# Two maxima per step ahead of the exponentials: a reordered attention stage on one core

## The reference, cut to what matters

```python
q = _rmsnorm(_rope(q), q_norm_w)
k = _rmsnorm(_rope(k), k_norm_w)
scores = jnp.einsum('bqgtd,bqgsd->bqgts', q, k) * scale
scores = jnp.where(mask[None, None, None], scores, NEG)
attn = jax.nn.softmax(scores, axis=-1)
out = jnp.einsum('bqgts,bqgsd->bqgtd', attn, v)
out = out.transpose(0, 3, 1, 2, 4).reshape(Bx, Tx, QPG * N_KV * D_HEAD)
return out @ wo.T
```

## Time and profile before

| | us |
|---|---|
| median of 3 runs (lowest, highest) | 1922.25 (1918.28, 1922.78) |
| profiled execution, its own time | 1921.04 |
| its span | 1919.1 |
| PE busy in the span | 1778.8 (93%) |
| DVE busy | 1530.7 (80%) |
| ACT busy | 1355.5 (71%) |
| POOL busy | 920.5 (48%) |

### The profile page before, as it was taken

The page is one execution under the profiler, slowest core; times in us unless marked ns, Lnnn a source line. Parts: engine busy times, 40 slices in busy tenths (PEclk is TensorE's granted clock), DMA queues, the critical chain, the costliest instruction groups (busy, mean ns, idle before and its releaser), DMA issues.

```text
span 1919.1 us, 35529 instructions
## 1 busy us (share of the span) xinstructions
PE 1778.8 (93%) x10789; PEld 1275.9 (66%) x10789; DVE 1530.7 (80%) x3377; ACT 1355.5 (71%) x3865; POOL 920.5 (48%) x1544
## 2 busy tenths in 40 slices
PE   3999999999999977999997999999999999989998
PEld 2777887887887866877775666666655665654443
DVE  5788888888888856567657899998999888986665
ACT  1567777677677653444445999999998999986765
POOL 1222322322322310032238999999898999983200
PEclk9999999999999988999997999999999999999999
DMA  3311111111111000000000000000000000004454
GB/s 98 95 44 40 34 45 39 34 45 39 34 45 39 25 1 1 1 1 1 1 1 1 2 2 2 2 2 2 2 2 1 2 2 2 2 7 177 189 216 165
DMA packets 30520, 69.05 MB, mean 36 GB/s; under 512 B 14108, under 2 KB 14748, under 8 KB 28028
## 3 DMA queue, kind: packets, MB, share of 16 engines
q1 hardware_dynamic: 30332, 66.78, 10.6%
HBM read 45.12 MB, written 2.36 MB: 25 GB/s over the span
## 4 chain that ended last, share of the span: by engine, by line
PE 33%; DVE 10%; ACT 9%; issue 6%; POOL 4%; DVEq 0%; ACTq 0%; POOLq 0%
ACT apb L1460 5%; PE ps L65 4%; PE ps L67 3%; PE ps L66 3%; PE ps L1218 3%; PE ps L1777 3%; PE ps L1201 3%; PE ps L1189 3%; PE ps L1228 2%; POOL apb L1574 1%; DVE atq L1281 1%; PE ps L1763 1%; PE ps L1184 1%; DVE amx L1321 1%; ACT aqT L1449 1%
## 5 line engine op out<-in xcount | busy, mean ns | idle before, releaser
L1460 ACT ACTIVATE apb<-ps,amx 128x128 f32<-128x128 f32 x1024 | 360.5, 369 | 23.6 <-DVE amx L1321 22.8
L1574 POOL TENSOR_TENSOR apb<-apb,arc 128x512 f32<-128x512 f32 x256 | 268.2, 1048 | 28.4 <-DVE arc L1329 27.4
L1460 ACT ACTIVATION_READ_ACCUMULATOR apb<-ps,amx 128x1 f32 x1024 | 214.4, 209 | 0.0
L1336 DVE COPY apT<-ps 128x512 f32<-128x512 f32 x256 | 172.6, 674 | 51.2 <-PE ps L1201 47.9
L583 POOL TENSOR_TENSOR h0h<-h0h,const 128x1 fp32r<-128x1 f32 x256 | 46.7, 218 | 338.8 <-DVE h0l L479 338.8
L65 PE MATMUL ps<-h0h,w123h 128*128 128x512 f32 x512 | 203.2, 397 | 0.0
L67 PE MATMUL ps<-h0h,w123l 128*128 128x512 f32 x512 | 202.5, 396 | 0.0
L66 PE MATMUL ps<-h0l,w123h 128*128 128x512 f32 x512 | 202.5, 395 | 0.0
L479 DVE SCALAR_TENSOR_TENSOR h0l<-ps,h0h 128x1024 fp32r<-128x1024 f32 x128 | 156.1, 1219 | 46.5 <-ACT h0h L383 46.5
L1201 PEld LDWEIGHTS ps<-const,apb 128*128 128x128 f32 x1024 | 109.8, 141 | 121.3 <-issue 90.9
L1321 DVE TENSOR_REDUCE amx<-ps 128x4 f32<-128x512 f32 x256 | 174.3, 681 | 4.6 <-PE ps L1189 4.3
(11 more groups left out here) (325 smaller groups left out, 5030.8 us busy)
## 6 DMA issues: line engine op xcount, KB each, us to landing
h<-gates SPq DMA_DIRECT2D x8, 2048.0 KB, 7.0
atq<-gates SPq DMA_DIRECT2D x8, 2048.0 KB, 7.0
x0k<-x0h SPq DMA_DIRECT2D x128, 72.0 KB
x<-in_x SPq DMA_DIRECT2D x32, 192.0 KB, 2.6
x0k<-x0l SPq DMA_DIRECT2D x64, 72.0 KB
x0k<-x0h SPq DMA_DIRECT2D x64, 48.0 KB
out<-akT SPq DMA_DIRECT2D x16, 128.0 KB, 1.9
x0k<-x0l SPq DMA_DIRECT2D x32, 48.0 KB
```

The source lines that it names most:

```text
L1336: ve.tensor_copy(pT[:, 4 * k:4 * k + 4, :], ps[:, TB, :].rearrange("p (h t) -> p h t", h=4)).then_inc(S["pT"], 1)
L1460: last = ac.activation(pb[:, i % 2, head, :], ps[:, SB[n % 3], h * T:(h + 1) * T], ACT.Exp, bias=mx[:, k, h:h + 1], accum_out=sm[:, i % 2, ...
L1574: po.tensor_tensor(p, p, rc[:, i % 2, 4 * k:4 * k + 4].unsqueeze(2).to_broadcast([T, 4, T]), ALU.mult).then_inc(S["pn"], 1)
```

## The change

Four edits. DVE takes both maxima of a step in the even slot, and in the odd slot the reciprocals of both slots, with the rotation between them; the sum of squares moves one slot on. ACT reads the rotated sum of the queries in SBUF (`qr`) for its squares, where it read the projection in PSUM, and waits for POOL's addition (`S["qr"]`) for it. On ACT the exponentials stand at the head of the odd slot, and in the even slot `keep_x` and the square come behind them. PE's projection waits for the rotation of the one before (`S["rope"]`), which is now the last to read the bank, where it waited for the square.

```diff
         def project(m):
             i, h = m // 2, m % 2
             if m >= 1:
-                pe.wait_ge(S["sq"], m)
+                pe.wait_ge(S["rope"], m)
...
-            if 0 <= u < PARTS:
-                maximum(u)
-            if 0 <= u - 1 < PARTS:
-                recip(u - 1)
+            if u % 2 == 0:
+                if 0 <= u < PARTS:
+                    maximum(u)
+                    maximum(u + 1)
+            else:
+                if 0 <= u - 1 < PARTS:
+                    recip(u - 1)
+                if u in at_q:
+                    rope_q(at_q[u])
+                if 0 <= u < PARTS:
+                    recip(u)
+                if u - 2 in at_q:
+                    sum_q(at_q[u - 2])
             if u in at_pt:
                 p_copy(at_pt[u])
-            if u in at_q:
-                rope_q(at_q[u])
-            if u - 1 in at_q:
-                sum_q(at_q[u - 1])
...
-            ac.wait_ge(S["rope"], m + 1)
+            ac.wait_ge(S["qr"], m + 1)
             if i >= 1:
                 ac.wait_ge(S["ssq"], m - 1)
-            ac.activation(sqb[:, h, :], ps[:, QB, :], ACT.Square).then_inc(S["sq"], 1)
+            ac.activation(sqb[:, h, :], qr[i % 2][:, h, :], ACT.Square).then_inc(S["sq"], 1)
...
+            if u % 2 == 1 and 0 <= u < PARTS:
+                exps(u)
             if u - 1 in at_pv:
                 keep_o(at_pv[u - 1])
-            if u - 1 in at_q:
-                square(at_q[u - 1])
             if u - 1 in at_qt:
                 keep_q(at_qt[u - 1])
             if u in at_rms:
                 rms_q(at_rms[u])
-            if u in at_xt:
-                keep_x(at_xt[u])
...
-            if 0 <= u < PARTS:
+            if u % 2 == 0 and 0 <= u < PARTS:
                 exps(u)
+            if u in at_xt:
+                keep_x(at_xt[u])
+            if u - 1 in at_q:
+                square(at_q[u - 1])
```

## The result

The changed kernel takes 1989.47 us (median of 4 runs, 1988.60 to 1990.28) against 1921.39 before (median of 4, with one run more than the table above): a ratio of 1.0357, with a 95% interval of 1.0339 to 1.0375. The forecast was 1988. The profiled execution spans 1988.3 us, 69.2 more than before. One single run in all that follows, of e7, was a slow one (2324.47 us at a granted clock of 0.745, where its others had 0.97), and e7's number is the median of its other three.

A forecast was written before the change was run, and what follows sets the result against it. It took a ring of four engines, ordered by handovers, to bound the attention stage. 43.7 + 2.07 + 0.49 + 0.87 + 0.4 gave a 47.5 us period against 43.3; times 15.9, +67 on 1921: 1988, range 1955 to 2015.

The forecast's parts named there:

- No instruction gained or lost, all is order: Attention stage: 256 maxima, 256 reciprocals and 128 squares stay as before; the change is only order and waits.
- The loop of 5.46 us a step through the second reciprocal: ACT and DVE: DVE's reciprocal awaits its own slot's exponentials, closing a loop of 5.46 us a step, 43.7 for eight.
- E0: ACT's exponentials of the even slot, 1.37 us in the loop's sum.
- E1: ACT's exponentials of the odd slot, 1.37 us in the loop's sum.
- Extras on the loop: Once a period: 2.07 DVE pieces, 0.49 copy of inputs, 0.87 unhidden ACT pieces, 0.4 late transposes; period 47.5 us.
- the stage's +67: Attention stage: a period longer by 4.2 us, times 15.9 periods, adds 67 us to the kernel's time.
- The square's slower read: ACT's square from SBUF instead of PSUM: +0.034 us a step, 4.4 us if on the ring, 0 if not.
- PE's removed waits give nothing: Projection's 18.3 us wait for squares goes, at most 1.3 us of PE a period; costed at zero gain.
- Small loss: Rival: DVE's part of the loop is hidden, ACT's path bounds; +0.7 a period, 1932 us; chance 0.10, in-between included.
- PE's clock: Rival, larger loss: a twentieth of the stage at half clock with PE 85% busy, +26 us, 2014; chance 0.10.
- The signs: Expected in the profile: periods 47 to 48 us, reciprocals waiting every step, logarithm waits near 0.6, PE waiting at L1218.
- The gain: Rival: PE, 93% busy, sets the ring, so its shrunken waits save 37 us, giving 1884; chance 0.03.

The follow-up runs named there:

- e7: The changed kernel with the query edit alone undone: square reads the projection in PSUM, projection waits for the square; 2068.96 us, ratio 1.0783.
- e2: The changed kernel with the second reciprocal moved to the next even slot, behind the two maxima; 1950.19 us, ratio 1.0154.
- e9: Kernel before with paired maxima, rotation early, odd-slot exponentials ahead of the logarithm pair, and both reciprocals in the odd slot around the rotation; 1933.20 us.
- e1: The changed kernel with the sum of squares put ahead of the second reciprocal on DVE in odd slots; 1959.63 us, ratio 1.0202.
- e6: The kernel before with the query edit alone: square reads SBUF and waits for POOL's addition, projection waits for the rotation; 2042.92 us, ratio 1.0647.
- e10: The changed kernel with the square of the queries cut into four 128x128 instructions, as a probe; 2015.44 us, ratio 1.0497.
- e3: The changed kernel with the copy of outputs put back ahead of the exponentials in the odd slot; 2039.42 us, ratio 1.0617.
- e11: The kernel before with only DVE's order changed: maxima paired in even slots, rotation ahead of reciprocal and copy in odd slots; 1902.74 us, ratio 0.9913.
- e8: Kernel before with paired maxima, reciprocals in the slot after their exponentials, rotation first in odd slots, odd-slot exponentials ahead of ACT's logarithm pair; 1902.34 us.
- e4: The changed kernel with the second reciprocal in the next even slot and the copy of outputs ahead of the odd slot's exponentials; 1938.51 us, ratio 1.0092.

## Why the prediction was right, point by point

- **No instruction gained or lost, all is order**: right. Busy times in the stage grew by 0.6 us (PE) to 11.7 (ACT); the stage grew by 62.
- **The loop of 5.46 us a step through the second reciprocal**: right. The step without extra pieces takes 5.46 from E0 to E0. Its pieces were right one by one: 2.17 us from E1 to E0 through DVE against 2.19. e2 and e9 take the reciprocal out of the loop and put it into another; 39 and 31 us go and come with it. e1 takes only the sum of squares out of it. That shortens this loop by 8 x 0.59 = 4.7 us a period, of which 1.9 (30 us of time) showed. The plain step took all of it, from 5.46 to 4.86, but three steps of the eight now stand at 5.83 to 6.12, and DVE's copies wait 46.5 us in 600 for PE's transposes, where they waited 30.0. PE's wait for the copy of outputs stayed, 52.8 us in 600.
- **Extras on the loop, 2.07 + 0.49 + 0.87, and 0.4 for copies that wait for transposes**: a little too large. The period came out at 47.0 to 47.1 against 47.5, so 3.35 for the extras where I had 3.83. The steps from E0 to E0 show which. The eight of a period take 5.95, 5.54, 5.78, 5.50, 6.18, 6.25, 6.36 and 5.46 us (medians over the stage). In four of them a piece shows at its price over 5.46: the copy of inputs 0.49, the sum for the keys 0.33 (5.78), the residual 0.79 (6.25), the statistics 0.90 (6.36), together 2.51 where I had 2.56. For the other two terms, 0.87 and 0.4, there is 0.84 left. The keys' logarithm pair and the copy of keys on ACT cost next to nothing, because they fall into steps in which DVE's extras make E0 wait for its maximum anyway:

```profile
1319.59 0.59 ACT L1428 ACTIVATE akT<-ps 128x512 f32<-128x512 f32 x1
1320.76 0.37 ACT L1465 ACTIVATE apb<-ps,amx 128x128 f32<-128x128 f32 x1 [0.58 <-DVE amx L1321]
```

  The copy of the output product and the late copy of turned weights fall into the same step, which is 0.72 longer. The forecast took only 0.21 off each piece on ACT, and overlooked that DVE's way has its own extras in two of the same steps.
- **What lies around the stage**: not forecast. The first scores come 4.9 us later and the tail is 2.4 longer. Why the first scores are late is not shown: with the query edit alone (e6) they come 7.0 us late, and with the new orders alone (e7) 6.9. These 7 us made up for the 5 by which the stage's +67 was too large; that 1988 came so close to 1989.5 is in this part luck.
- **The square's slower read**: 641 ns (median) for both of its sources, against 599 from PSUM: +42, where I took +34 from another function's row. From one start to the next, which is what the loop pays, it is 520 ns against 493, +27. By e10's 69% that is some 2 us of the 68 (127 x 0.027 x 0.69), an estimate. The Trainium skill (Perfetto Trace Analysis, Optimizing Scalar/DVE Operations) gives overheads of about 93 ns on SBUF and 51 on PSUM and calls them engine-busy times. Their difference, 42, is what the durations of this case show; from start to start the squares show less. But e6 shows that I priced the wrong half of this edit: the read is cheap, the wait for POOL's addition is what can cost 120 us, and it is nothing only because the square was moved as well.
- **PE's removed waits give nothing**: right. They went from 32.4 to 0.6 us, and e3 shows that even removing the one that took their place makes things worse. That holds for this order: in e11 PE's wait for squares goes and 18 us with it.
- **Small loss** (DVE's part hidden, ACT alone the bound, 1932): fallen. ACT waits for a maximum 76 times in 600 us, each time with E0, so DVE's way is the longer one, and its extras do not hide. In the timeline ACT stands 0.17 us for it.
- **PE's clock**: fallen. It was 1.00 from 1060 to 1700 us, with PE busy 85% and single waits of its matmuls of up to 1.1 us for the copy of outputs.
- **The signs**: as forecast, but for one size. ACT's logarithm waits for the sum of squares in every step, 46.2 us in 102 steps, 0.45 each, where I had near 0.6.
- **The gain**: fallen for this order. But the reason that I gave against it, that PE does not set the ring, holds only for the changed order. e8 and e11 show 18 us to be had from DVE's order, and PE is then busy 632.3 of 675.0 us, 94%.

What stays open: e4 has undone both causes and is still 18.5 us slower than before. Its first scores come 6.0 us late and its stage is 707.3 us against 694.5. What is left of the change in it is the query edit with the square behind E0, the logarithm pair behind E1, the sum of squares one slot on, and the rotation ahead of the copy; I did not take these apart.

## What to carry to other kernels

Where engines with in-order queues feed each other in a ring, look in every queue for an instruction that needs what another engine makes in the same slot, and write down the loop that it closes: what stands behind it until the partner's next input, plus the partner's work. Its length in start-to-start times, against the present period, told gain from loss here before any busy share did. It tells less of how much a shorter loop gives back: a term of 4.7 us a period gave 1.9 (e1), since the next way through PE then set the pace in some steps. And price a removed wait only by what is behind it in the ring: the largest wait of PE's matmuls (L1218, 56 us) was worth minus 50 us in one order and plus 12 in another.

## What was not expected of the hardware

Four 128x128 ACT instructions out of SBUF on end took 0.80 us to the next start, 0.20 each, while an exponential of that size takes 0.25 to its accumulator read and 0.09 more for the read. I had taken the 0.25 for the price of any instruction of that size.
